# Attention: where the sums of the diagonal score blocks stand in VectorE's order

## The reference, cut to what matters

```python
scores = einsum('bnhd,bmhd->bhnm', q, k) / sqrt(Dh)        # causal
att_t  = softmax(scores where same or previous segment)     # "terrace" window
out_t  = einsum('bhnm,bmhd->bhnd', att_t, v)
att    = softmax(scores)                                    # full causal rows
awc    = att.reshape(b, H, r, seg, L) * exp(index_decays)
pcs    = awc.sum(axis=-2)                                   # weighted column sums per segment
# pcs is decayed over segments, normalised, and weights the sums over k v^T
```

## Time and profile before

| | us |
|---|---|
| median of the timed runs | 2776.61 |
| profiled execution, its own time | 2764.8 |
| its span, first to last instruction | 2763.1 |
| TensorE matmuls busy | 2328.3 (84%) |
| VectorE busy | 1957.2 (71%) |
| ScalarE busy | 1550.6 (56%) |
| GpSimd busy | 1215.6 (44%) |
| the 128 diagonal sums, busy | 86.6 |

### The profile page before, as it was taken

One profiled execution on the slowest core, in us unless ns is written; L12 is line 12 of the kernel. 1 busy time (PEld: TensorE's weight loads), 2 busy tenths in 40 slices (PEclk: granted clock), 3 DMA queues, 4 the chain that ended last, 5 costly groups with the idle time before them and its releaser, 6 DMA issues. The chain is left out here.

```text
span 2763.1 us, 72877 instructions
## 1 busy us (share of the span) xinstructions
PE 2328.3 (84%) x27200; PEld 1545.7 (56%) x27200; DVE 1957.2 (71%) x4914; ACT 1550.6 (56%) x3595; POOL 1215.6 (44%) x2134
## 2 busy tenths in 40 slices
PE   8689999999999999997797944399999999678792
PEld 5444444444444444444655844277777777555681
DVE  6478888887888888884473656167777776467465
ACT  5467777776777777773252322266666665235230
POOL 3323333333333333335574536444444444237561
PEclk9879999998999999998898965599999999789896
DMA  6711111111112111112327645301111110632555
GB/s 219 239 38 34 35 37 37 37 37 26 36 37 64 37 37 37 37 37 71 146 102 196 230 156 194 112 28 45 49 49 49 49 49 26 215 144 97 158 155 202
DMA packets 187129, 247.69 MB, mean 90 GB/s; under 512 B 41128, under 2 KB 144437, under 8 KB 184864
## 3 DMA queue, kind: packets, MB, share of 16 engines
q1 hardware_dynamic: 160384, 186.33, 21.8%
q0 software_dynamic: 19872, 50.41, 5.3%
q10 hardware_dynamic: 6528, 6.31, 0.8%
HBM read 136.12 MB, written 110.73 MB: 89 GB/s over the span
## 5 line engine op out<-in xcount | busy, mean ns | idle before, releaser
L588 ACT ACTIVATE at_E<-at_S,at_mn 128x1024 f32<-128x1024 f32 (+4 forms) x704 | 591.5, 848 | 233.1 <-DVE at_mn L658 233.1
L658 DVE TENSOR_REDUCE at_mn<-at_S 128x1 f32<-128x1024 f32 (+4 forms) x704 | 612.4, 878 | 127.7 <-PE at_S L768 123.2
L808 PE MATMUL at_pcs<-at_E,at_c 128*32 128x256 f32 (+1 forms) x4864 | 445.1, 353 | 0.0
L768 PE MATMUL at_S<-at_sk,at_sq 96*128 96x512 bf16 (+3 forms) x1152 | 341.2, 361 | 49.0 <-ACT at_E L588 47.7
L540 POOL TENSOR_TENSOR at_kvo<-at_kh,at_vh 128x256 f32<-128x256 f32 x512 | 303.6, 627 | 0.1
L808 PEld LDWEIGHTS at_pcs<-at_E,at_c 128*32 128x32 f32 x4864 | 188.7, 110 | 91.3 <-issue 84.8
L520 POOL TENSOR_TENSOR at_fi<-at_f,at_inv 128x12 f32<-128x12 f32 x128 | 26.3, 206 | 427.1 <-DVE at_inv L675 427.1
L1250 POOL DMA_INDIRECT expert_out<-m_ysb,m_dst x158 | 155.4, 984 | 131.6 <-DVE m_dst L1428 117.7
L808 PE MATMUL at_pcs<-at_Tt,at_c 128*32 128x128 f32 x1024 | 211.5, 289 | 0.0
L578 ACT ACTIVATE at_Tt<-at_S,at_mn 128x192 f32<-128x192 f32 x512 | 173.2, 421 | 64.7 <-DVE at_mn L648 64.2
L768 PEld LDWEIGHTS at_S<-at_sk,at_sq 96*128 96x128 bf16 x1152 | 78.9, 98 | 229.4 <-issue 101.3
(11 more groups left out here) (373 smaller groups left out, 5506.3 us busy)
## 6 DMA issues: line engine op xcount, KB each, us to landing
m_xg<-expert_rows SPq DMA_DIRECT2D x158, 129.0 KB
at_sq<-q_parts SPq DMA_DIRECT2D x192, 64.0 KB, 2.3
at_sk<-k_parts SPq DMA_DIRECT2D x192, 64.0 KB, 2.2
memory_rows<-m_blank SPq DMA_DIRECT2D x8, 1032.0 KB, 4.4
gl_hx<-memory_rows SPq DMA_DIRECT2D x32, 258.0 KB, 3.7
m_wgu<-in_f_wgu SPq DMA_DIRECT2D x2, 4096.0 KB, 14.0
rt_yin<-expert_out SPq DMA_DIRECT2D x8, 1024.0 KB, 8.9
fn_yin<-expert_out SPq DMA_DIRECT2D x8, 1024.0 KB, 10.4
```

What stands on the lines that cost most here:

```text
L588: nc.scalar.activation(E[:, at:at + w], S[v % NS_B][:, 0:w], ACT.Exp, bias=mn[:, q, s, 1 + j:2 + j], scale=-1.0, accum_out=rs[:, q, s, 1 + ...
L658: nc.vector.tensor_reduce(mn[:, q, s, 1 + j:2 + j], S[v % NS_B][:, 0:w], AX.X, ALU.min).then_inc(s_mn, 1)
L768: ins = nc.tensor.matmul(S[v % NS_B][:, c:c + cw], sq[:, u, t * P:(t + 1) * P], sk[:, u, c0 + c:c0 + c + cw], start=True, stop=True)
L808: ins = nc.tensor.matmul(pcs[j * R:(j + 1) * R, cols[0]:cols[1]].rearrange("p (b c) -> p b c", c=P), lhsT, rhs, start=(n, j) not in touche ...
```

## The change

`diag_sums` of a quad is issued behind `tops` and, where there is one, `normalise`; for the first quad behind `tops`.

```diff
             window_minima(0)
             for k in range(1, 1 + len(units[0])):
                 minima(0, k)
+            tops(0)
             diag_sums(0)
-            tops(0)
             for g in range(NG):
...
                     if k == 3:
                         inverses(g)
                         outputs(g)
-                    if k == 4:
-                        diag_sums(g + 1)
                 tops(g + 1)
                 if n and q == 3:
                     normalise(n - 1)
+                diag_sums(g + 1)
             normalise(NHEAD - 1)
```

## The result

| | before | after |
|---|---|---|
| median of the timed runs, us | 2776.19 (2773.03 to 2782.9, 6 runs) | 2761.89 (2759.32 to 2765.02, 6 runs) |
| ratio | | 0.9942, 95% 0.9929 to 0.9956 |
| profiled execution, us | 2764.8, span 2763.1 | 2763.46, span 2761.7 |
| mean granted clock of TensorE in it | 0.910 | 0.919 |

The change makes the kernel 0.58% faster, 14 us; I had forecast 2783 within 2767 to 2802. Both need an explanation.

What follows compares the result with a forecast made beforehand. No engine was full; hand-overs between TensorE, VectorE and ScalarE bound it. Per lap (one head), 0.08 - 0.33 + 0.31 to 0.19 - 0.21 + 0.31, middle 0.2, times 31 gave 6 us: 2783, range 2767 to 2802.

Steps and rivals of the forecast that it cites:

- (A): From q1 to q2: window block 0.45 to 0.56 late, mostly slack; q2's k3 comes 0.08 to 0.19 us late.
- (B): From q2 to q3: k5 and k6 start earlier, smaller GpSimd collision; q3's k3 comes 0.33 to 0.21 us early.
- (C): From q3 through q0 to q1: all 0.59 paid, slack takes 0.28; q1's k3 comes 0.31 us late.
- Absorbed (1): Rival: the lap is TensorE's and the window block's delay falls wholly into waits; 2777 us, chance 0.20.
- Faster (2): Rival: earlier k5 releases scores k1 sooner in q2 and q3; lap -0.39, -12 us, 2765 us, chance 0.15.
- (3): Rival, clearly slower: no slack between exponentials and scores k3; 1.04 a lap, +32 us, 2809 us, chance 0.12.
- (4): Rival: GpSimd keeps VectorE out for its whole run of products; 0.7 a lap, +22 us, 2799 us, chance 0.05.

Runs made afterwards that it cites:

- r6: Kernel before with the diagonal sum moved in q1 alone: 2796.91 us, ratio 1.0059 to before.
- r5: Kernel before with the diagonal sum moved in q2 alone: 2766.37 us, ratio 0.9951 to before.
- r13: Kernel before, no sum moved, with idle matmuls ahead of the window block, five in q2 and four in q3: 2744.38 us, ratio 0.9892 to before.
- r16: r5 with one idle mask matmul added ahead of q2's window block: 2736.83 us, ratio 0.9859 to before.
- r10: Kernel before with q1's and q2's sums moved, their transposes doubled and five idle matmuls in q2's window: 2755.29 us, ratio 0.9883 to before.

## Why the prediction was wrong

**(A) q1 to q2: right.** k3 to k3 is 904.55 - 896.06 = 8.49, before 8.39: +0.10, forecast 0.08 to 0.19. r6 has it alone, with +0.12 a lap.

**(B) q2 to q3: right.** 913.00 - 904.55 = 8.45, before 8.79: -0.34, forecast -0.33 to -0.21. The differences took 0.26 instead of 0.60, as worked out. r5 alone: -0.32.

**(C) q3 to q0 to q1: mis-sized by 0.5.** 931.32 - 913.00 = 18.32, before 17.51: +0.81 against +0.31. From `kvn` to k3 it is 4.08 against 3.77, the +0.31 forecast. The 0.5 is in front of `kvn`: 14.24 from q3's k3 instead of 13.74, where I had it back at its time since the sum no longer stood ahead of it. But without that sum q0's differences come earlier against GpSimd's run of products: before they started 1.66 into the run and took 0.17; now GpSimd's run starts at 925.14 and they start 1.20 in, just behind the second product of 0.59, and wait for the third to end.

```profile
925.14 2.96 POOL L540 TENSOR_TENSOR at_kvo<-at_kh,at_vh 128x256 f32<-128x256 f32 x5
```

In (B) I had weighed just such a collision, and didn't look for the next one. So the lap came out at +0.58, outside my +0.06 to +0.29, and by itself this would have made 31 x 0.58 = 18 us, 2795 in my terms and inside the range.

**The failing step** is the sentence "Some laps run at a lower clock [...] I don't correct for it", and with it the median carried over 12 us above the profiled run. I treated the 0.97 of the earlier trace rows as a property of the stretch that only hides work, when it was a few long heads that the change could take away. The wait of 1.16 and that of 0.95 stood in the earlier trace rows and in the forecast, as idle time of TensorE; what they also set off, no step asked. What stands in its place: the falls took 20.5 us in before's profile, and r13, which has before's lap and no falls, is 1.1%, some 30 us, faster than before. As an estimate for the timed runs, if all the 11.4 us by which they lie above the profile are falls too, that is 32; less the 17 of longer laps it leaves 15, and 14 were measured.

**Rivals.** Absorbed (1) did not hold: the lap changed. Faster (2) named the right fact, scores k1 released earlier, and came nearest in time (2765), but for a shorter lap that did not come: by its own mechanism the number is luck. (3) would have given +1.04 a lap; at q1 only 0.10 of 0.45 came through, so the slack is real. (4) would have put q3's k3 some 0.3 late: it came 0.34 early, and q0's differences ended at 926.96, while GpSimd's run went on to 928.10.

The Trainium skill, page "TensorE: Matmul & The Clock Gate", section "A second HAM failure mode: psum-queue depth-cycling", tells of a kernel whose short rests between groups of matmuls make the clock swing between its two levels. The runs agree in kind, and r13 to r16 show by the falls at each place that it is the rests themselves; I didn't weigh it in the forecast.

## What to carry to other kernels

Before working out an edit's gain, list every lap of the profile: where some are longer, the first question is what the granted clock does in them and which wait stands ahead of each fall. A price worked out lap by lap is only half of the sum when the edit also changes a wait of the engine that the clock is granted to. And when an instruction goes from ahead of a VectorE operation with two SBUF inputs, look again at where that operation then meets GpSimd's products.

## What the runs showed of the hardware

- In these kernels the granted clock fell to half, for 7 or 10 us, about 2 us after a rest of TensorE of 0.95 to 1.17 us, in the middle of dense work; not after the same rest when it was cut to 0.40 or less (q3), or to 1.04 or less (q2).
- Useless matmuls in the rests paid: nine a head brought 1.1% (r13), one a head 30 us (r5 to r16, 2766.37 to 2736.83).
- The mean busy share of TensorE doesn't tell whether falls come at the two places: none at 1088.5 (r10), at 1049.0 (r16) and at 1038.8 (after) busy us of 1120, seven at 1049.2 (before).
- VectorE's differences, which read two SBUF inputs, got in behind one GpSimd product and not behind its whole run: they took 0.62 instead of 0.17, 0.45 more, of at most one product's 0.59, while the run of products went on (profile after, 926.34). In before's q2 the wait was 0.43, for the last product of a run.
